# Joint classifier: its head rearranged by single q pieces, pairs of p23 and a q without v0n

## The reference, cut to what matters

```python
variables = [softmax(p, axis=-1) for p in split(logits, 4)]      # 512 rows, 4 variables of 16 states
joint = variables[0]
for v in variables[1:]:
    joint = einsum('b...,ba->b...a', joint, v)
flat = joint.reshape(B, -1)                                      # 512 x 65536
num_y_joint = einsum('bj,by->yj', flat, y_true)                  # 100 classes
num_joint = sum(flat, axis=0)
prob = clip(maximum(num_y_joint, 1e-6) / maximum(num_joint, 1e-6), 0, 1)
probs = einsum('yj,bj->by', prob, flat)
```

## Time and profile before

| | before |
|---|---|
| median of 3 runs | 535.99 us (535.52 to 536.15) |
| profiled execution, its own time | 535.51 us |
| its span | 533.6 us |
| PE / VectorE / ScalarE / GpSimd busy | 99% / 55% / 8% / 4% |
| instructions | 8648 |

### The profile page before, as it was taken

The page is one execution under the profiler, slowest core; times in us unless marked ns, Lnnn a source line. Parts: engine busy times, 40 slices in busy tenths (PEclk is TensorE's granted clock), DMA queues, the critical chain, the costliest instruction groups (busy, mean ns, idle before and its releaser), DMA issues.

```text
span 533.6 us, 8648 instructions
## 1 busy us (share of the span) xinstructions
PE 529.6 (99%) x3125; PEld 305.1 (57%) x3125; DVE 295.8 (55%) x763; ACT 41.2 (8%) x95; POOL 22.8 (4%) x20
## 2 busy tenths in 40 slices
PE   9999999999999999999999999999999999999997
PEld 5555555555555555555555555555555555555555
DVE  7896766764575444444467544444446544444446
ACT  6950000000200000000020000000001000000000
POOL 0000000000040000000022000000004000000000
PEclk9999999999999999999999999999999999999999
DMA  2854334330000000000000000000000000000000
GB/s 51 144 89 79 53 68 79 41 59 1 1 0 1 1 0 0 0 0 0 1 0 1 1 0 0 0 0 0 0 0 1 1 0 0 0 0 0 1 1 17
DMA packets 34771, 9.21 MB, mean 17 GB/s; under 512 B 34496, under 2 KB 34752, under 8 KB 34752
## 3 DMA queue, kind: packets, MB, share of 16 engines
q1 hardware_dynamic: 34224, 8.73, 9.2%
q10 hardware_dynamic: 528, 0.20, 0.2%
HBM read 0.34 MB, written 0.20 MB: 1 GB/s over the span
## 4 chain that ended last, share of the span: by engine, by line
PE 99%; DVE 0%; issue 0%; POOL 0%; DVEq 0%; POOLq 0%
PE joined L445 16%; PE numbers L437 16%; PE joined L447 16%; PE joined L446 16%; PE numbers L438 16%; PE numbers L439 16%; PE numbers L461 1%; PE numbers L464 1%; PE numbers L467 1%; PE numbers L470 1%; DVE acc L404 0%; PE joined L540 0%; PE joined L545 0%; PE joined L542 0%; POOL idle L175 0%
## 5 line engine op out<-in xcount | busy, mean ns | idle before, releaser
L446 PE MATMUL joined<-r_lo,pt_hi 128*128 128x400 f16 x504 | 167.6, 332 | 0.0
L447 PE MATMUL joined<-r_hi,pt_lo 128*128 128x400 f16 x504 | 167.6, 332 | 0.0
L445 PE MATMUL joined<-r_hi,pt_hi 128*128 128x400 f16 x504 | 167.5, 332 | 0.0
L437 PE MATMUL numbers<-q_hi,p_hi 128*128 128x404 f16 x496 | 166.1, 335 | 0.0
L439 PE MATMUL numbers<-q_hi,p_lo 128*128 128x404 f16 x496 | 165.3, 333 | 0.0
L438 PE MATMUL numbers<-q_lo,p_hi 128*128 128x404 f16 x496 | 165.2, 333 | 0.0
L323 DVE TENSOR_SCALAR den<-numbers 128x4 f32<-128x4 f32 x128 | 20.7, 162 | 212.4 <-PE numbers L439 211.4
L335 DVE SCALAR_TENSOR_TENSOR r_lo<-ratio,r_hi 128x400 f16<-128x400 f32 x128 | 78.4, 612 | 4.4
L328 DVE SCALAR_TENSOR_TENSOR ratio<-numbers,inv 128x400 f32<-128x400 f32 x128 | 73.5, 575 | 4.4
L446 PEld LDWEIGHTS joined<-r_lo,pt_hi 128*128 (+1 forms) x504 | 49.2, 98 | 36.3
L445 PEld LDWEIGHTS joined<-r_hi,pt_hi 128*128 (+1 forms) x504 | 49.1, 97 | 36.3
(11 more groups left out here) (47 smaller groups left out, 81.0 us busy)
## 6 DMA issues: line engine op xcount, KB each, us to landing
pt_hi<-p_hi SPq DMA_TRANSPOSE x16, 3.1
pt_lo<-p_lo SPq DMA_TRANSPOSE x16, 3.2
labels<-in_r_y_true_dram ACTq DMA_DIRECT2D x1, 200.0 KB, 2.9
out_dram<-acc SPq DMA_DIRECT2D x1, 150.0 KB, 1.8
x<-in_r_logits_dram SPq DMA_DIRECT2D x1, 128.0 KB, 2.2
out_dram<-acc SPq DMA_DIRECT2D x1, 50.0 KB, 1.5
```

Of the source, the lines that this page charges most:

```text
L437: pe.matmul(out, p_at(p_hi, tile, k), q_at(q_hi, g, k), start=(k == 0), stop=False)
L445: pe.matmul(out, p_at(pt_hi, tile, k), r_hi[:, slot, :], start=first, stop=False)
L446: pe.matmul(out, p_at(pt_hi, tile, k), r_lo[:, slot, :], start=False, stop=False)
L447: last = pe.matmul(out, p_at(pt_lo, tile, k), r_hi[:, slot, :], start=False, stop=final)
```

## The change

- `p23` is made by pairs of k, all (c, d) at once: first k = 0 and 1, later k = 2 and 3. So `p_hi` of k = 0 and 1 needs one instruction of VectorE instead of two.
- `v0n` is no longer made in the head. ScalarE scales e0 and e1 together (`v01s`), and q comes from one three-operand instruction, labels * `whole` * scaled e0 (`make_q`), in four pieces. GpSimd makes `v0n` from the same two after the last `p_lo`, for `v0f`.
- The labels are loaded by SP's queue behind the logits, and no longer by ScalarE's.
- The idle turns are 18, 6, 4 and 3 (31 instead of 41), the last three behind the first q.
- The 48 first matmuls stand in a new order. `numbers` of tile 0 ends with lo\*hi of k=3. The join of tile 0 takes r_lo before pt_lo and waits for pt_hi alone first (a semaphore of its own, `first_landed`). The count of tile 4 takes its eight matmuls with `p_hi` first and its four with `p_lo` last.

```diff
-        IDLE_START, IDLE_EXPS, IDLE_V0 = 22, 10, 9
-        Q_PARTS = 3
+        IDLE_START, IDLE_EXPS, IDLE_V0, IDLE_Q = 18, 6, 4, 3
+        Q_PARTS, QL_PARTS = 4, 3
...
             sp.dma_start(x[:, :, :], ...).then_inc(logits_in, 16)
+            sp.dma_start(labels[:, :, 0:CLASSES], ...).then_inc(labels_in, 16)
...
             pool.wait_ge(p_ready, KC * S)
+            pool.tensor_tensor(v0n[:, :, :], v01s[:, :, 0, :], whole[:, :].unsqueeze(2).broadcast_to([LANES, KC, S]),
+                               ALU.mult).then_inc(v0n_made, 1)
...
-            act.dma_start(labels[:, :, 0:CLASSES], ...).then_inc(labels_in, 16)
...
             act.wait_ge(exps, 2)
-            act.activation(v1s[:, :, :], ek[:, :, 1, :], ACT.Copy, scale=UP).then_inc(v1s_made, 1)
-            act.wait_ge(p23_made, 2)
+            act.activation(v01s[:, :, :, :], ek[:, :, 0:2, :], ACT.Copy, scale=UP).then_inc(v01s_made, 1)
+            act.wait_ge(p23_made, 1)
             first_p_hi(0, 0)
             first_p_hi(0, 1)
             make_first_q_hi(1, 0, 1)
             first_p_hi(1, 0)
             make_first_q_hi(2, 1, 2)
             first_p_hi(1, 1)
+            act.wait_ge(p23_made, 2)
             first_p_hi(0, 2)
+            make_first_q_hi(3, 2, 3)
             first_p_hi(0, 3)
-            make_first_q_hi(3, 2, 4)
+            make_first_q_hi(4, 3, 4)
             first_p_hi(1, 2)
             first_p_hi(1, 3)
...
+            def make_q(k, group):
+                v0g = v01s[:, k, 0, group * AG:(group + 1) * AG].unsqueeze(2).broadcast_to([LANES, AG, CW])
+                yk = labels[:, k, :].unsqueeze(1).broadcast_to([LANES, AG, CW])
+                dve.scalar_tensor_tensor(qf[:, k * NW:(k + 1) * NW].rearrange("p (a y) -> p a y", a=AG),
+                                         yk, whole[:, k:k + 1], v0g, ALU.mult, ALU.mult).then_inc(q_made, 1)
...
             pe.wait_ge(idle_set, 1)
             idle_turns(IDLE_START)
-            pe.wait_ge(p23_made, 2)
+            pe.wait_ge(p23_made, 1)
             idle_turns(IDLE_EXPS)
-            pe.wait_ge(v0n_made, 1)
+            pe.wait_ge(whole_made, 1)
             idle_turns(IDLE_V0)
+            pe.wait_ge(q_made, 1)
+            idle_turns(IDLE_Q)
...
-            pe.wait_ge(pt_landed[0], 32)
+            pe.wait_ge(first_landed, 16)
             pe.wait_ge(r_hi_made, 1)
...
+            fifth = numbers[0][:, 0:NW]
+            pe.wait_ge(p_hi_made, p_count(2))
+            for k in range(KC):
+                pe.matmul(fifth, p_at(p_hi, SLOTS, k), q_at(q_hi, 0, k), start=(k == 0), stop=False)
+                pe.matmul(fifth, p_at(p_hi, SLOTS, k), q_at(q_lo, 0, k), start=False, stop=False)
+            pe.wait_ge(p_ready, p_count(2))
```

More of the change, by code:

```diff
@@ L77, in joint_classifier @@
         v0f = sb("v0f", [LANES, KC, S], FP32)
-        v1s = sb("v1s", [LANES, KC, S], FP32)
+        v01s = sb("v01s", [LANES, KC, 2, S], FP32)
         labels = sb("labels", [LANES, KC, CW], FP32)
@@ L142, in joint_classifier, with landings @@
         block = ctx.enter_context(nc.Block())
+        def landings(i):
+            return (i // TURN_SEMS + 1) * 32 - (16 if i % TURN_SEMS == 0 else 0)
         def p_count(i):
@@ L150, in _ @@
             sp.dma_start(x[:, :, :], logits.rearrange("(p k) (v s) -> p (k v) s", k=KC, s=S)).then_inc(logits_in, 16)
+            sp.dma_start(labels[:, :, 0:CLASSES], y_true.rearrange("(p k) y -> p k y", k=KC)).then_inc(labels_in, 16)
             def turn(out, src, i):
@@ L159, in _ @@
                 if i >= TURN_SEMS:
-                    sp.wait_ge(landed, i // TURN_SEMS * 32)
+                    sp.wait_ge(landed, landings(i - TURN_SEMS))
                 sp.wait_ge(p_hi_made, p_count(i))
-                turn(pt_hi, p_hi, i).then_inc(landed, 16)
+                turn(pt_hi, p_hi, i).then_inc(landed if i else first_landed, 16)
                 sp.wait_ge(p_ready, p_count(i))
@@ L207, in p_hi_chunk @@
                                       p23[:, k, :].rearrange("p (h n) -> p h n", n=HALF),
-                                      ACT.Copy, scale=v1s[:, k, bass.ds(i, 1)])
+                                      ACT.Copy, scale=v01s[:, k, 1, bass.ds(i, 1)])
             def first_p_hi(i, k):
@@ L288, in start_q @@
             def start_q(g, k):
-                dve.wait_ge(q_ready, Q_PARTS + (g - 2) * KC + k + 1 if g > 1 else min(k + 1, Q_PARTS))
-                v0_times_y(k, k + 1, g)
+                dve.wait_ge(q_ready, QL_PARTS + (g - 2) * KC + k + 1 if g > 1 else min(k + 1, QL_PARTS))
+                make_q(k, g)
             def finish_q(g, k):
@@ L303, in p_lo_chunk @@
                 return dve.scalar_tensor_tensor(lo[:, :, k, :], p23[:, k, :].rearrange("p (h n) -> p h n", n=HALF),
-                                                v1s[:, k, bass.ds(i, 1)], hi[:, :, k, :], ALU.mult, ALU.subtract)
+                                                v01s[:, k, 1, bass.ds(i, 1)], hi[:, :, k, :], ALU.mult, ALU.subtract)
             def first_p_lo(i, k, made):
@@ L345, in _ @@
             dve.wait_ge(reduced, 2)
[L346 to L350, removed]
+            dve.reciprocal(whole[:, :], whole[:, :]).then_inc(whole_made, 1)
+            dve.wait_ge(whole_made, 1)
+            dve.wait_ge(v01s_made, 1)
             dve.wait_ge(labels_in, 16)
             dve.wait_ge(ones_set, 1)
-            v0_times_y(0, 1, 0)
-            v0_times_y(1, 2, 0)
+            make_q(0, 0)
             first_p_lo(0, 0, 1)
+            make_q(1, 0)
+            make_p23(2, 4)
             first_p_lo(0, 1, 2)
-            v0_times_y(2, 4, 0)
             finish_first_q(1, 0, 1)
+            make_q(2, 0)
             finish_first_q(2, 1, 2)
+            make_q(3, 0)
             first_p_lo(1, 0, 3)
@@ L497, in _ @@
             hi_hi(3, 1)
-            pe.wait_ge(q_ready, 1)
-            for tile in range(4):
-                hi_lo(tile, 0)
+            hi_lo(2, 0)
+            hi_lo(3, 0)
+            pe.wait_ge(p_hi_made, 5)
+            pe.wait_ge(q_hi_made, 3)
+            hi_hi(0, 2)
+            hi_hi(1, 2)
             pe.wait_ge(q_ready, 2)
@@ L504, in _ @@
             pe.wait_ge(p_hi_made, 6)
[L505 to L508, removed]
+            pe.wait_ge(q_hi_made, 4)
+            hi_hi(0, 3)
+            hi_hi(1, 3)
             pe.wait_ge(p_ready, 3)
@@ L521, in _ @@
             lo_hi(1, 2)
-            pe.wait_ge(p_ready, 6)
[L523 to L528, removed]
+            pe.wait_ge(p_hi_made, 7)
+            hi_hi(2, 2)
+            hi_hi(3, 2)
+            pe.wait_ge(q_ready, 3)
+            hi_lo(0, 2)
+            hi_lo(0, 3)
+            pe.wait_ge(p_ready, 6)
+            lo_hi(0, 3, True).then_inc(numbers_ready, 1)
+            hi_lo(1, 2)
+            hi_lo(1, 3)
+            lo_hi(1, 3, True).then_inc(numbers_ready, 1)
+            pe.wait_ge(p_hi_made, 8)
+            hi_hi(2, 3)
+            hi_hi(3, 3)
             for tile in range(2, 4):
@@ L531, in _ @@
                 hi_lo(tile, 3)
+            pe.wait_ge(p_ready, 7)
+            lo_hi(2, 2)
+            lo_hi(3, 2)
             pe.wait_ge(p_ready, 8)
-            for tile in range(2, 4):
-                lo_hi(tile, 2)
-                lo_hi(tile, 3, True).then_inc(numbers_ready, 1)
-            pe.wait_ge(pt_landed[0], 32)
+            lo_hi(2, 3, True).then_inc(numbers_ready, 1)
+            lo_hi(3, 3, True).then_inc(numbers_ready, 1)
+            pe.wait_ge(first_landed, 16)
             pe.wait_ge(r_hi_made, 1)
@@ L540, in _ @@
                 pe.matmul(joined[k][:, 0:PW], p_at(pt_hi, 0, k), r_hi[:, 0, :], start=True, stop=False)
-            for k in range(KC):
-                pe.matmul(joined[k][:, 0:PW], p_at(pt_lo, 0, k), r_hi[:, 0, :], start=False, stop=False)
             pe.wait_ge(ratios_ready, 1)
@@ L545, in _ @@
                 pe.matmul(joined[k][:, 0:PW], p_at(pt_hi, 0, k), r_lo[:, 0, :], start=False, stop=False)
[L547 to L551, removed]
+            pe.wait_ge(pt_landed[0], landings(0))
+            for k in range(KC):
+                pe.matmul(joined[k][:, 0:PW], p_at(pt_lo, 0, k), r_hi[:, 0, :], start=False, stop=False)
+            fifth = numbers[0][:, 0:NW]
+            pe.wait_ge(p_hi_made, p_count(2))
+            for k in range(KC):
+                pe.matmul(fifth, p_at(p_hi, SLOTS, k), q_at(q_hi, 0, k), start=(k == 0), stop=False)
+                pe.matmul(fifth, p_at(p_hi, SLOTS, k), q_at(q_lo, 0, k), start=False, stop=False)
+            pe.wait_ge(p_ready, p_count(2))
+            for k in range(KC):
+                last = pe.matmul(fifth, p_at(p_lo, SLOTS, k), q_at(q_hi, 0, k), start=False, stop=(k == KC - 1))
+            last.then_inc(numbers_ready, 1)
+            for tile in range(1, TILES - SLOTS):
+                if tile % 2 == 0:
+                    pe.wait_ge(pt_landed[tile // 2 % TURN_SEMS], landings(tile // 2))
+                join(0, tile, tile % SLOTS)
                 if tile % 2 == 0:
```

38 lines of the change are left out of this document (16 added, 22 removed).

## The result

| | before | changed |
|---|---|---|
| median | 535.64 us (22 runs) | 534.97 us (22 runs) |
| fastest to slowest | 535.41 to 536.34 | 534.83 to 535.32 |
| profiled execution, its own time | 535.51 | 535.27 |
| its span | 533.6 | 533.2 |

The ratio is 0.9987, 95% interval 0.9981 to 0.9993: 0.67 us off the median, where 0.79 had been forecast, and within the 0.2% that counted as no change. The slowest run came down by 1.0 us, the fastest by 0.6.

The account below looks back on a forecast made before the run. PE, 99% busy, was taken to bound the kernel, with only the head able to move. Gains of 0.64 us there and 0.15 from the labels made 0.79: 535.99 to 535.2 us, range 534.6 to 535.9.

Parts of the forecast that it names:

- Way through the head: VectorE's and PE's new order up to tile 4: the 48 matmuls end at 15.35, tile 4 starts 0.64 us earlier.
- the two PE waits: PE gaps in the head: 0.10 us before the 11th matmul (q_lo of k=0), 0.16 before the 17th (`q_hi` of k=2).
- First matmul: Head chain to PE's first needed matmul: one `p23` instruction and `v0n` leave it, start at 6.86 us, gain 0.81.
- They hold nobody up: PE's idle turns in the head: the last three start from 6.1 to 6.4 us, before the first needed matmul at 6.86.
- rival 1: Head without PE gaps, logits 0.3 us early: gain 1.22 us, 534.8 us; chance 0.27.
- Labels: Labels behind the logits on SP's queue: logits land earlier, 0.15 us taken, bounds 0 and 0.3.
- Join of tile 0: PE's join behind the 48 matmuls: starts at 15.35, ends at 17.37; pt_lo lands at 15.9, wanted at 16.7.
- The number: Whole kernel: median 535.99 us less 0.79 gives 535.2 us, within 0.2% of no change; chance 0.55.
- a dear q: Rival in VectorE's head: the new q costs more; at 0.6 us more each, 537.6 us; chance 0.04.
- Rival 2: Head before tile 4: a piece arrives late, PE waits 0.4 to 0.7 us more, 535.6 to 535.9 us; chance 0.14.

## Why the prediction was right, and where it was not

- **Way through the head: right.** The layout of VectorE and ScalarE held to 0.02 us from one row to the next. Where the turns don't hold, the two PE waits and the start of tile 4 came out as laid down: 17.30 + 2.05 = 19.35 against 20.06 before, 0.71 us, which is 0.64 and the 0.07 by which these logits landed earlier.
- **First matmul: right as a price, wrong as a general case.** "They hold nobody up" was said of the idle turns, from one profile whose clock rose at 4.5 us, and their number was put at nothing in the sum. In other executions the rise is later, and the turns hold. The profiled run started at 7.30 instead of 6.76, and its tile 4 at 17.54 instead of 17.3; fewer turns alone were worth 0.18 us of the median. The remark under rival 1, that a late rise is worth up to 0.17 us to the change, was the right mechanism: the same cut of ten turns took 0.18 off the median of the kernel before and 0.7 off its slowest runs. The Trainium skill ("TensorE: Matmul & The Clock Gate", Part 1) has the rise differ between runs; the profiles agree, with 4.3 to 6.9 us in eleven of them and 10.4 in the twelfth. One reading under rival 1 is off: the 41 turns of the profile before have 0.32 us to spare in their two waits, not 0.42 (start to start 0.23 and 0.31, where turns without a wait have 0.11).
- **Labels: the failed term.** 0.15 us was forecast; the landings differ by 0.06 on average, and moving the labels' load changed the spans in neither kernel. The two queues do share the engines at 2.1 to 2.3 us, but the landing varies by 0.2 us from run to run. The forecast's lower bound, 0, was nearer.
- **Join of tile 0: a sentence that was wrong.** "Asked for second, as before, it would have been wanted at 16.0, in time by 0.1 only": the kernel before waits for both transposes ahead of the whole join (`pt_landed[0]` at 32), so it would have been wanted at 15.35 and cost some 0.5. The run with the old order measured 0.56. This edit is what lets the others arrive.
- **The number: near in part by luck.** The sum was 0.64 for the head and 0.15 for the labels. The runs have next to nothing for the labels and 0.18 for the idle turns, which the sum had at nothing; and of the 0.64 some 0.15 does not reach the time (below). What was left out nearly makes up for what is missing: 0.64 + 0.18 - 0.15 = 0.67, a rough balance over several batches.
- **Rivals.** No profile showed a dear q in the head (0.64 us); the two of 1.4 us in the main loop stand beside GpSimd's work, as before. Rival 2, a further wait ahead of tile 4, did not appear; rival 1's gapless PE did, but because the turns had made it late.

By medians, taken over several batches: of 0.67 us, 0.18 is fewer idle turns. The rest, 0.50 between the kernel before with 31 turns and the changed one, needs the new join order (0.56 when undone) and holds the p23 by pairs (0.22), the q without v0n (0.05, not clear of noise) and the labels (nothing). These overlap and don't add up.

**Open.** Own time less span is 1.8 to 1.9 us in the three profiles of the old head and 2.0 to 2.1 in the eight others and the changed kernel's. The single runs say the same: 1.90 us on average in 86 runs of the kernel before, 2.05 in the 22 of the changed one. So 0.1 to 0.2 us of what the head gains inside the span does not reach the time. It isn't the labels (2.00 on average with them moved back, 1.82 with them moved alone); what it is was not tried.

## What to carry to other kernels

An earlier start is worth only what the last piece due behind it allows: follow every wait up to the point where the engine is dense for good, and reorder the work there first. Work put in to bring a clock up must be sized for executions in which the clock rises late: too much of it holds the first needed instruction, too little leaves needed work to the lower clock. Both show as spread between runs before they show in a median. One profile has one moment of the rise, so read the spread of the runs beside it.

## What was not expected of the hardware

The rise of PE's clock came at 4.3 to 6.9 us in eleven profiles of nearly the same head, and at 10.4 in the one with 22 turns. It has to be read from the durations of equal matmuls (0.421 us, then 0.272): the profile's granted clock says 1.00 in every microsecond from 1 to 10, in the kernel before, in the changed one and with 22 turns. With 41 turns and no rest the runs spread over 1.6 us, with 31 over 0.5, and with 22 turns and four rests of about 0.5 us they fell into two groups 1.1 us or more apart.
